# Mixture of 8: weights and biases split inside the router, identity products, one-row memset moved

## The chip, the cores and the metric

The kernel runs on one core of one Trainium2 chip. The metric is the device time of one execution in microseconds; times of several runs are compared by their medians.

## The reference

Two layers of a perceiver run over 128 sequences of 32 tokens with 128 numbers each: attention to a context, self-attention with a feed-forward part, and a mixture of experts. The change concerns the last part of layer 0, a mixture of 8 experts with two chosen per token, on the layer-normalised tokens x (4096 rows, 128 columns):

```
scores = softmax(x @ gate_w.T)                       # 8 scores a token
for each of the two experts e with the largest scores, of score w:
    h  = silu((w * x) @ w1[e].T + b1[e])
    x2 = h @ w2[e].T + b2[e]
    x3 = (w * x) @ w3[e].T + b3[e]
    out += x2 * x3
out += (silu(x @ sw1.T) * (x @ sw2.T)) @ sw3.T       # shared expert
```

The result is added to the rows before normalisation. (The kernel takes x @ w1[e].T + b1[e] / w for all experts and applies w afterwards as a scale, which is why the inverted scores have to be ready before the wide products, and in two parts.)

## The kernel before, in words

All 4096 rows stay on chip as 32 tiles of 128 rows by 128 columns. The engines run programs of their own, ordered by semaphores written out by hand; there is no planner. Layer 0's mixture of 8 is `stage_moe0` (from L1742). It has a router, a short passage, and a loop over tiles.

**Start.** SyncE issues the loads: `gate` and `lower` on semaphore `g_in`, then w1, w3, the biases `braw`, and sw12, turn_m, w2, sw3, all seven on `w_in` (L1803 to L1806); then it waits, and issues the next stage's loads (L1810). VectorE works out means and inverse deviations of all rows (L102 to L112), with one square root on ScalarE (L118). GpSimd begins with a memset of one row of 3084 numbers in a buffer of the next stage (L2120), then makes a tile of ones (L2122, L2124).

**Router.** It goes in 8 groups of 4 tiles. VectorE normalises two tiles of a group (L123, called at L1960), ScalarE the other two (L1909). TensorE transposes the four (L1876), ScalarE copies them to `xf` (L1915), TensorE multiplies them by the gate (L1819, 8 columns a tile) one group behind. The transposed tiles are needed in two parts, a high part rounded to the matmul's format and the rest: GpSimd writes the high part (L2092), VectorE the low one (L1965). Two groups are in flight.

**Weights.** Weights w1, w3 and three bias rows (1024 columns each, the biases' second part in 32 partitions) are split in the same way. This starts behind the router: ScalarE rounds them (L1942, L1944), GpSimd subtracts (L2129, L2134).

**Passage.** VectorE takes the maximum of the 8 logits (L2047), subtracts it (L2049), ScalarE takes the exponential (L1946), VectorE normalises to scores (L2051 to L2057), inverts them (L2059), and lays them out in three parts (L2061 to L2065). The semaphore `st` counts these ten steps; the score is step 6. TensorE transposes the result (L1884), ScalarE copies it (L1949), GpSimd makes the first two tiles' operands (L2095, L2099), VectorE meanwhile ranks the experts of the first four tiles (L1975 to L1993). TensorE does the shared expert's first products (L1833) and the wide products of tile 0 (L1826 to L1829).

**Loop.** For each of 32 tiles TensorE transposes the hidden values (L1843), multiplies by sw3 (L1850), does the next tile's wide and shared products, and the second matrices (L1860, L1862). GpSimd sums and prepares the tile after the next.

The later mixture of 32 experts (layer 1, `stage_moe1`) has a router of the same form, and it already issues products of the identity with itself at its start and one in each group, with the helper `keep_clock` (L1687). The names of its lines: products L1687, transposes L2529, gate products L2486. Their results go to a part of the accumulator memory that nothing reads.

Of the kernel before, what the change touches and what calls it, by code (L numbers as in the profile page):

```python
# [12 lines left out]
F32 = mybir.dt.float32  # L13
# [1728 lines left out]
def stage_moe0(nc, k, w, next_loads, next_ones):  # L1742

    ED, NG, G4 = E0 * D, T // 4, 4 * E0
    with ExitStack() as ctx:
# [31 lines left out]
        next_in, row_ok = sem("next_in"), sem("row_ok")  # L1777
        H1, X3, HT, UP, ZO = 0, 2, 4, 6, 7
        X_B, L_B, R_B = 0, 2, 4
        loads = [(w1, w["w1"]), (w3, w["w3"]), (braw, w["braw"]), (sw12, w["sw12"]),   # L1780
                 (turn_m, w["turn_m"]), (w2, w["w2"]), (sw3, w["sw3"])]
        LOADED = 16 * len(loads)
# [19 lines left out]
        def _(sp):  # L1802
            sp.dma_start(gate[:, :], w["gate"]).then_inc(g_in, 16)  # L1803
            sp.dma_start(lower[:, :, :], w["lower"]).then_inc(g_in, 16)
            for dst, src in loads:
                sp.dma_start(dst[:], src).then_inc(w_in, 16)  # L1806
            sp.wait_ge(g_in, 32)
            sp.wait_ge(w_in, LOADED)
# [5 lines left out]
        def _(pe):  # L1814
# [54 lines left out]
            pe.wait_ge(g_in, 32)  # L1869
            for g in range(NG):  # L1870
                if g > 1:
                    pe.wait_ge(xf_ok, g - 1)
# [7 lines left out]
            route(NG - 1)  # L1880
            pe.wait_ge(st, 10)
            pe.wait_ge(zero_ok, 1)
            for g in range(NG):
# [9 lines left out]
            pe.wait_ge(bl_ok, 3)  # L1893
# [5 lines left out]
            wide_up(X3, 1, 0, x3_mm)  # L1899
            groups(pe, step)  # L1900

        @block.scalar
        def _(act):
# [36 lines left out]
            act.wait_ge(w_in, LOADED)  # L1940
            for n, src in enumerate((w1, w3)):
                nc.scalar.copy(wide[:, 2 * n, :], src[:, :]).then_inc(wh_ok, 1)  # L1942
            for n in range(3):
                nc.scalar.copy(bias[:, n, :], braw[:, n, :]).then_inc(bh_ok, 1)  # L1944
            act.wait_ge(st, 2)
            nc.scalar.activation(lg[:, :, :], lg[:, :, :], ACT.Exp).then_inc(ex_ok, 1)  # L1946
            for b in range(2):
                act.wait_ge(rp_mm, b + 1)
                nc.scalar.copy(rpT[:, 4 * b:4 * b + 4, :], four(R_B + b)).then_inc(rp_ok, 1)  # L1949
# [5 lines left out]
        def _(dve):  # L1955
# [69 lines left out]
            def ranking(i, t0, base):  # L2025
# [6 lines left out]
                else:  # L2032
# [5 lines left out]
                                           ALU.mult).then_inc(sh_set, 1)  # L2038
            normal(0)
            for g in range(NG):  # L2040
                if g < NG - 1:
                    normal(g + 1)
                low(g)
# [27 lines left out]
            kept(0, 0)  # L2071
            shared(0)
# [16 lines left out]
        def _(pool):  # L2089
# [30 lines left out]
            nc.gpsimd.memset(next_ones, 1.0).then_inc(row_ok, 1)  # L2120
            pool.wait_ge(row_ok, 1)
# [5 lines left out]
            for n, src in enumerate((w1, w3)):  # L2127
                pool.wait_ge(wh_ok, n + 1)
# [712 lines left out]
```

## Time and profile before

| | |
|---|---|
| median of 3 runs | 2665.84 us (2662.67 to 2671.37) |
| the profiled execution | 2661.88 us |
| its span | 2660.1 us |
| granted TensorE clock, mean | 0.966 |
| TensorE busy | 2482.2 us |
| VectorE busy | 1610.0 us |
| ScalarE busy | 1418.8 us |
| GpSimd busy | 1049.4 us |

The span goes from the first to the last instruction of the profiled execution; the execution's own time is 1.8 us longer. Times in rows count from the span's start. PE is TensorE's matmuls, DVE VectorE, ACT ScalarE, POOL GpSimd. A line of a timeline merges instructions of one kind that follow each other: start, busy time, engine, line, operation, what it writes and reads, how many; in brackets the idle time ahead and who ended it. A product of 32-bit operands stands there as two records, a transpose as one. A clock of 1.00 is 2.4 GHz, 0.50 is 1.2 GHz.

### The profile page before, as it was taken

The page shows a single profiled execution, that of the slowest core. Times are in us where ns is not written, and L with a number is a line of the kernel's source. Part 1 is how long each engine was busy: PE and PEld are TensorE (multiplying, and loading weights), DVE is VectorE, ACT ScalarE, POOL GpSimd, SP SyncE. Part 2 cuts the span into 40 slices and gives each one's busy share as a digit, 9 for nine tenths or more (in the row PEclk, how much of TensorE's full clock was granted, in tenths as well). Part 3 has the DMA queues.
Part 4 walks back from the last instruction along what each step waited for, and adds up shares of the span by engine and source line. Part 5 has one row for each costly group of instructions (what it writes and reads, how often), then busy time and mean ns, then how long its engine had stood idle before and what let it go on. Part 6 is the DMA issues. An engine that isn't in the chain of part 4 may idle for free. (4 is left out here: it accounts for less than half of the span.)

```text
span 2660.1 us, 92957 instructions
## 1 busy us (share of the span) xinstructions
PE 2482.2 (93%) x38497; PEld 2096.3 (79%) x38497; DVE 1610.0 (61%) x3115; ACT 1418.8 (53%) x3839; POOL 1049.4 (39%) x1152
## 2 busy tenths in 40 slices
PE   6999999999989999997679998999999989889999
PEld 5888888888877888885469986777777768778888
DVE  3555555555567777775655554777777747544553
ACT  3555555555556667674644444777777734422222
POOL 2333333333340000002344444666666623345555
PEclk9999999999999999998869998999999989789999
DMA  6322222222134111110020000210101010065563
GB/s 201 128 89 89 89 89 89 89 89 89 67 125 170 40 47 39 47 40 2 1 71 1 0 0 23 50 30 24 30 24 30 13 52 0 3 135 111 107 136 75
DMA packets 60190, 168.35 MB, mean 63 GB/s; under 512 B 6429, under 2 KB 20385, under 8 KB 55209
## 3 DMA queue, kind: packets, MB, share of 16 engines
q1 hardware_dynamic: 60074, 166.71, 21.2%
q8 instruction: 84, 1.38, 0.2%
q14 instruction: 32, 0.26, 0.0%
HBM read 145.18 MB, written 21.51 MB: 63 GB/s over the span
## 5 line engine op out<-in xcount | busy, mean ns | idle before, releaser
L566 POOL TENSOR_TENSOR l_probs<-l_probs,l_rden 128x1024 f32<-128x1024 f32 x128 | 242.2, 1892 | 428.8 <-DVE l_rden L424 428.8
L508 ACT ACTIVATE l_probs<-ps,l_nmax 128x257 f32<-128x257 f32 x512 | 236.0, 474 | 226.4 <-DVE l_nmax L418 226.4
L967 POOL TENSOR_TENSOR l_probs<-l_probs,l_rden 128x1024 f32<-128x1024 f32 x128 | 242.3, 1893 | 171.2 <-DVE l_rden L818 171.2
L418 DVE TENSOR_REDUCE l_nmax<-ps 128x2 f32<-128x514 f32 x256 | 165.5, 688 | 217.4 <-PE ps L303 217.4
L903 ACT ACTIVATE l_probs<-ps,l_nmax 128x257 f32<-128x257 f32 x512 | 236.0, 474 | 59.9 <-DVE l_nmax L812 59.9
L2723 POOL TENSOR_TENSOR m_hh<-m_hh,m_cb 128x512 f32<-128x512 f32 (+1 forms) x136 | 177.3, 1304 | 156.6 <-DVE m_hh L2675 138.5
L303 PE MATMUL ps<-l_ctxQ,l_q 32*128 32x257 f32 x3072 | 202.6, 392 | 7.1 <-ACT l_probs L508 6.4
L2581 ACT ACTIVATE m_sg<-ps 128x512 f32<-128x512 f32 (+1 forms) x136 | 81.3, 598 | 231.6 <-PE ps L138 230.8
L812 DVE TENSOR_REDUCE l_nmax<-ps 128x2 f32<-128x514 f32 x256 | 165.4, 688 | 61.1 <-PE ps L704 57.6
L2675 DVE TENSOR_TENSOR m_hh<-ps,m_sg 128x512 f32<-128x512 f32 (+1 forms) x136 | 94.0, 691 | 178.6 <-PE ps L138 159.0
L823 DVE COPY l_pT<-ps 128x512 f32<-128x512 f32 x256 | 164.9, 686 | 52.2 <-PE ps L713 48.0
L343 PE MATMUL ps<-l_pT,l_ctxK 128*32 128x128 f32 x6144 | 194.3, 275 | 0.8 <-DVE l_pT L461 0.8
L343 PEld LDWEIGHTS ps<-l_pT,l_ctxK 128*32 128x32 f32 x6144 | 159.9, 110 | 43.2 <-issue 42.0
L303 PEld LDWEIGHTS ps<-l_ctxQ,l_q 32*128 32x128 f32 x3072 | 145.0, 184 | 32.2 <-ACT l_probs L508 13.8
L2517 PEld LDWEIGHTS ps<-m_wd,m_hh 128*128 128x128 f32 (+1 forms) x1088 | 143.0, 193 | 26.4 <-issue 15.1
L2517 PE MATMUL ps<-m_wd,m_hh 128*128 128x128 f32 (+1 forms) x1088 | 145.4, 277 | 12.0 <-POOL m_hh L2723 12.0
L1422 POOL CAST enc_xt<-enc_xs 128x256 fp32r (+1 forms) x32 | 12.8, 401 | 364.2 <-PE ps L138 364.2
L330 PE MATMUL ps<-ident,l_probs 128*128 128x128 f32 x1024 | 139.8, 279 | 1.4 <-ACT l_U L514 1.2
L713 PE MATMUL ps<-ident,l_probs 128*128 128x128 f32 x1024 | 133.2, 273 | 0.8 <-DVE x L832 0.4
L330 PEld LDWEIGHTS ps<-ident,l_probs 128*128 128x128 f32 x1024 | 109.6, 141 | 26.9 <-issue 25.0
L521 ACT COPY l_q<-ps 128x512 f32<-128x512 f32 x96 | 56.2, 585 | 126.7 <-PE ps L253 126.7
L461 DVE COPY l_pT<-ps 128x512 f32<-128x512 f32 x128 | 88.5, 692 | 52.3 <-PE ps L330 52.3
(371 smaller groups left out, 6471.1 us busy)
## 6 DMA issues: line engine op xcount, KB each, us to landing
l_ctxQ<-in_ctx_q SPq DMA_DIRECT2D x32, 1542.0 KB, 6.5
m_cb<-combined SPq DMA_DIRECT2D x32, 768.0 KB, 13.8
enc_dash<-kept SPq DMA_DIRECT2D x32, 512.0 KB, 3.3
l_ctxT<-in_ctx_t SPq DMA_DIRECT2D x32, 385.5 KB, 3.3
l_ctxK<-in_ctx_k SPq DMA_DIRECT2D x32, 384.0 KB, 3.1
m_cb<-combined SPq DMA_DIRECT2D x16, 512.0 KB, 13.5
kept<-enc_va SPq DMA_DIRECT2D x10, 512.0 KB, 3.2
kept<-enc_qsq SPq DMA_DIRECT2D x6, 512.0 KB
```

The costliest lines, as they stand in the source:

```text
L303: last_i = nc.tensor.matmul(ps[:, S_B + hg, 0:NK], q1[r:r + N, j, c, b, :], ctxQ[r:r + N, j, c, b * NK:b * NK + NK], start=c == 0, stop=c ...
L330: last_i = nc.tensor.transpose(ps[:, T_B + kt, hg * P:hg * P + P], probs[:, b, hg, kt * P:kt * P + P], k.ident[:, :])
L343: last_i = nc.tensor.matmul(ps[N * hg:N * hg + N, O_B, c * P:c * P + P], ctxK[:, j, at_k:at_k + N], pT[:, kt, P * hg:P * hg + P], start=kt ...
L418: nc.vector.tensor_reduce(nmax[:, par, 2 * half:2 * half + 2], ps[:, S_B + 2 * half:S_B + 2 * half + 2, 0:NK], AX.X, ALU.max, negate=True) ...
L508: nc.scalar.activation(probs[:, par, hg, :], ps[:, S_B + hg, 0:NK], ACT.Exp, bias=nmax[:, par, hg:hg + 1], accum_out=den[:, par, hg:hg + 1 ...
L566: nc.gpsimd.tensor_tensor(pr, pr, rden[:, b, :, None].to_broadcast([P, HG, NK - 1]), ALU.mult).then_inc(norm_ok, 1)
L812: nc.vector.tensor_reduce(nmax[:, b, 2 * half:2 * half + 2], ps[:, S_B + 2 * half:S_B + 2 * half + 2, 0:NK], AX.X, ALU.max, negate=True).t ...
L823: nc.vector.tensor_copy(pT[:, b % 2, kt, :], ps[:, T_B + kt, :]).then_inc(pt_ok, 1)
L903: nc.scalar.activation(probs[:, b, hg, :], ps[:, S_B + hg, 0:NK], ACT.Exp, bias=nmax[:, b, hg:hg + 1], accum_out=den[:, b, hg:hg + 1]).the ...
L967: nc.gpsimd.tensor_tensor(pr, pr, rden[:, b, :, None].to_broadcast([P, HG, K_W]), ALU.mult).then_inc(norm_ok, 1)
L2517: last = nc.tensor.matmul(ps[:, ACC + g % 2, n * P:n * P + D], hh[0:rows, v % 3, n * P:n * P + P], wd[0:rows, c, :], start=c + n == 0, sto ...
L2723: nc.gpsimd.tensor_tensor(h, h, cb[0:rows, c, :], ALU.mult).then_inc(h_ok, 1)
```

## The change

All edits are in `stage_moe0`.

- w1, w3 and the biases get a semaphore of their own, `first_in`, so that they can be used before the other loads are in. The order of the loads is as before.
- TensorE issues 8 identity products ahead of the router, one at the start of each group, and 6 behind the router when step 6 of `st` is done.
- ScalarE rounds w1 behind the turned copy of group 2 and w3 behind that of group 4; only the bias b2 is rounded behind the exponential.
- GpSimd rounds the biases b1 and b3 behind its high parts of groups 2 and 3 and subtracts for w1 and w3 behind those of groups 4 and 5.
- VectorE takes the low parts two groups later, subtracts for the two biases in iterations 5 and 6, and takes the last two low parts behind the ranking.
- GpSimd's low part of b2 and the one-row memset come behind the operands of the first two tiles. TensorE waits for that low part (`b2_lo`) ahead of the loop, and for two instead of three bias parts ahead of the wide products.

```diff
+        first_loads = [(w1, w["w1"]), (w3, w["w3"]), (braw, w["braw"])]
+        loads = [(sw12, w["sw12"]), (turn_m, w["turn_m"]), (w2, w["w2"]), (sw3, w["sw3"])]
...
             pe.wait_ge(g_in, 32)
+            keep_clock(nc, k, ZO, 8)
             for g in range(NG):
+                keep_clock(nc, k, ZO, 1)
                 if g > 1:
                     pe.wait_ge(xf_ok, g - 1)
...
             route(NG - 1)
+            pe.wait_ge(st, 6)
+            pe.nop(nofuse=True)
+            keep_clock(nc, k, ZO, 6)
             pe.wait_ge(st, 10)
             pe.wait_ge(zero_ok, 1)
+            pe.nop(nofuse=True)
...
-            pe.wait_ge(bl_ok, 3)
+            pe.wait_ge(bl_ok, 2)
...
             wide_up(X3, 1, 0, x3_mm)
+            pe.wait_ge(b2_lo, 1)
             groups(pe, step)
...
                 turned(g)
-            act.wait_ge(w_in, LOADED)
-            for n, src in enumerate((w1, w3)):
-                nc.scalar.copy(wide[:, 2 * n, :], src[:, :]).then_inc(wh_ok, 1)
-            for n in range(3):
-                nc.scalar.copy(bias[:, n, :], braw[:, n, :]).then_inc(bh_ok, 1)
+                if g == 2:
+                    act.wait_ge(first_in, FIRST)
+                    nc.scalar.copy(wide[:, 0, :], w1[:, :]).then_inc(wh_ok, 1)
+                if g == 4:
+                    nc.scalar.copy(wide[:, 2, :], w3[:, :]).then_inc(wh_ok, 1)
             act.wait_ge(st, 2)
             nc.scalar.activation(lg[:, :, :], lg[:, :, :], ACT.Exp).then_inc(ex_ok, 1)
+            nc.scalar.copy(bias[:, 1, :], braw[:, 1, :]).then_inc(b2_hi, 1)
...
+            def bias_low(n, done):
+                dve.wait_ge(bh_ok, done)
+                nc.vector.tensor_tensor(bias[N:2 * N, n, :], braw[N:2 * N, n, :], bias[N:2 * N, n, :].bitcast(F32),
+                                        ALU.subtract).then_inc(bl_ok, 1)
+
             normal(0)
             for g in range(NG):
                 if g < NG - 1:
                     normal(g + 1)
-                low(g)
+                if g > 1:
+                    low(g - 2)
+                if g == 5:
+                    bias_low(0, 1)
+                if g == 6:
+                    bias_low(2, 2)
...
             kept(0, 0)
+            low(NG - 2)
+            low(NG - 1)
             shared(0)
...
-            nc.gpsimd.memset(next_ones, 1.0).then_inc(row_ok, 1)
-            pool.wait_ge(row_ok, 1)
+            def wide_low(n, src):
+                pool.wait_ge(wh_ok, n + 1)
+                nc.gpsimd.tensor_tensor(wide[:, 2 * n + 1, :], src[:, :], wide[:, 2 * n, :].bitcast(F32),
+                                        ALU.subtract).then_inc(wl_ok, 1)
...
             for g in range(NG):
                 high(g)
...
+                if g == 2:
+                    pool.wait_ge(first_in, FIRST)
+                    nc.gpsimd.tensor_copy(bias[:, 0, :], braw[:, 0, :]).then_inc(bh_ok, 1)
+                if g == 3:
+                    nc.gpsimd.tensor_copy(bias[:, 2, :], braw[:, 2, :]).then_inc(bh_ok, 1)
+                if g == 4:
+                    wide_low(0, w1)
+                if g == 5:
+                    wide_low(1, w3)
+            pool.wait_ge(xl_ok, 1)
+            pool.wait_ge(w_in, LOADED)
             pool.wait_ge(rp_ok, 2)
             for t in range(2):
                 tile_in(t, t)
                 turn_in(0, t, t)
+            pool.wait_ge(b2_hi, 1)
+            pool.wait_ge(xt_ok, 2)
+            pool.wait_ge(rt_ok, 2)
+            nc.gpsimd.tensor_tensor(bias[N:2 * N, 1, :], braw[N:2 * N, 1, :], bias[N:2 * N, 1, :].bitcast(F32),
+                                    ALU.subtract).then_inc(b2_lo, 1)
+            pool.wait_ge(b2_lo, 1)
+            nc.gpsimd.memset(next_ones, 1.0).then_inc(row_ok, 1)
+            pool.wait_ge(row_ok, 1)
+            pool.wait_ge(xl_ok, NG)
             groups(pool, step)
```

## Rows read from the trace of the kernel before

**Rows 1.** The page: the span, and the engines' busy time.
```profile
span 2660.1 us, 92957 instructions
...
PE 2482.2 (93%) x38497; PEld 2096.3 (79%) x38497; DVE 1610.0 (61%) x3115; ACT 1418.8 (53%) x3839; POOL 1049.4 (39%) x1152
```

**Rows 2.** Stretches: length, busy us by engine, TensorE clock, DMA share, GB/s.
```profile
1330.20:1331.50 1.30, 0.00 (x0) 0.00 (x0) 1.30 (x3) 0.00 (x0) 1.30 (x1) 0.50 0.26 47
1342.00:1352.00 10.00, 10.00 (x51) 10.00 (x50) 4.31 (x10) 4.85 (x11) 2.45 (x4) 0.50 0.36 96
1366.50:1370.40 3.90, 3.13 (x13) 2.76 (x14) 2.07 (x6) 1.17 (x2) 1.15 (x4) 0.50 0.00 0
...
1450.00:1500.00 50.00, 50.00 (x334) 45.06 (x333) 27.41 (x42) 21.47 (x61) 23.52 (x38) 1.00 0.00 0
2299.20:2302.00 2.80, 2.77 (x13) 2.80 (x14) 2.23 (x13) 2.14 (x4) 0.00 (x0) 0.50 0.01 3
2302.30:2303.00 0.70, 0.70 (x9) 0.70 (x8) 0.06 (x1) 0.70 (x2) 0.00 (x0) 1.00 0.00 0
```

**Rows 3.** Timeline, start of the mixture of 8: start us, busy us, engine line.
```profile
1329.35 2.66 POOL L2120 MEMSET l_ctxT<- 1x3084 f32 x1 [3.12 <-POOLq L85]
...
1330.07 1.98 DVE L106 TENSOR_SCALAR mean<-half 128x32 f32<-128x32 f32 x1
...
1333.09 1.11 DVE L123 TENSOR_SCALAR m_xn<-x,mean,rstd 128x128 f32<-128x128 f32 x4
...
1334.23 1.94 PE L1876 MATMUL ps<-ident,m_xn 128*128 128x128 f32 x8 [28.41 <-DVE m_xn L123]
```

**Rows 4.** Timeline, start of the second mixture's router.
```profile
2299.23 3.68 PE L1687 MATMUL ps<-ident 128*128 128x128 f32 x18 [1.10 <-PEq L2164]
...
2299.76 0.18 DVE L106 TENSOR_SCALAR mean<-half 128x32 f32<-128x32 f32 x1
...
2301.25 1.11 DVE L123 TENSOR_SCALAR m_xn<-x,mean,rstd 128x128 f32<-128x128 f32 x4
```

**Rows 5.** Timeline, first router: transposes, high and low parts, weight subtractions.
```profile
1336.00 0.61 POOL L2092 CAST m_xs<-m_xf 128x512 fp32r<-128x512 f32 x1 [3.38 <-ACT m_xf L1915]
...
1340.71 0.69 DVE L1965 TENSOR_TENSOR m_xs<-m_xf,m_xs 128x512 fp32r<-128x512 f32 x1 [1.41 <-POOL m_xs L2092]
1340.74 1.09 PE L1876 MATMUL ps<-ident,m_xn 128*128 128x128 f32 x4
...
1350.55 1.09 PE L1876 MATMUL ps<-ident,m_xn 128*128 128x128 f32 x4
...
1353.29 4.89 POOL L2129 TENSOR_TENSOR m_wide<-m_w,m_wide 128x1024 fp32r<-128x1024 f32 x2 [0.35 <-ACT m_wide L1942]
```

**Rows 6.** Timeline, second router: transposes of two groups.
```profile
2306.33 0.63 PE L2529 MATMUL ps<-ident,m_xn 128*128 128x128 f32 x4 [0.92 <-issue]
...
2311.57 0.60 PE L2529 MATMUL ps<-ident,m_xn 128*128 128x128 f32 x4
```

**Rows 7.** Timeline, after the router: ScalarE, VectorE and GpSimd.
```profile
1354.06 2.94 ACT L1944 CAST m_bias<-m_braw 128x1024 fp32r<-128x1024 f32 x3
...
1355.36 0.42 DVE L2049 TENSOR_TENSOR m_lg<-ps,m_mx 128x256 f32<-128x256 f32 x1
1357.02 1.28 ACT L1946 ACT_TABLE_LOAD   x1
...
1358.34 7.16 POOL L2134 TENSOR_TENSOR m_bias<-m_braw,m_bias 32x1024 fp32r<-32x1024 f32 x3
...
1359.60 1.35 DVE L2055 TENSOR_TENSOR m_lg<-m_lg,m_mx 128x256 f32<-128x256 f32 x1
1360.99 2.31 DVE L2057 TENSOR_SCALAR m_score<-m_lg 128x256 f32<-128x256 f32 x1
```

**Rows 8.** Timeline, from the turned weights to the first loop step.
```profile
1366.50 1.97 PE L1884 MATMUL ps<-ident,m_rp 128*128 128x128 f32 x8 [11.63 <-DVE m_rp L2065]
...
1376.02 1.04 PE L1843 MATMUL ps<-ident,m_z 128*128 128x128 f32 x8
```

More of the change, by code:

```diff
@@ L1777, in stage_moe0 @@
         next_in, row_ok = sem("next_in"), sem("row_ok")
+        first_in, b2_hi, b2_lo = sem("first_in"), sem("b2_hi"), sem("b2_lo")
         H1, X3, HT, UP, ZO = 0, 2, 4, 6, 7
         X_B, L_B, R_B = 0, 2, 4
-        loads = [(w1, w["w1"]), (w3, w["w3"]), (braw, w["braw"]), (sw12, w["sw12"]),
-                 (turn_m, w["turn_m"]), (w2, w["w2"]), (sw3, w["sw3"])]
-        LOADED = 16 * len(loads)
+        first_loads = [(w1, w["w1"]), (w3, w["w3"]), (braw, w["braw"])]
+        loads = [(sw12, w["sw12"]), (turn_m, w["turn_m"]), (w2, w["w2"]), (sw3, w["sw3"])]
+        LOADED, FIRST = 16 * len(loads), 16 * len(first_loads)
         both = lambda pair: ps[:, pair:pair + 2, :].rearrange("p a b -> p (a b)")
@@ L1804, in _ @@
             sp.dma_start(lower[:, :, :], w["lower"]).then_inc(g_in, 16)
+            for dst, src in first_loads:
+                sp.dma_start(dst[:], src).then_inc(first_in, 16)
             for dst, src in loads:
@@ L1807, in _ @@
             sp.wait_ge(g_in, 32)
+            sp.wait_ge(first_in, FIRST)
             sp.wait_ge(w_in, LOADED)
@@ L2126, in _ @@
                 high(g)
-            for n, src in enumerate((w1, w3)):
-                pool.wait_ge(wh_ok, n + 1)
-                nc.gpsimd.tensor_tensor(wide[:, 2 * n + 1, :], src[:, :], wide[:, 2 * n, :].bitcast(F32),
-                                        ALU.subtract).then_inc(wl_ok, 1)
-            pool.wait_ge(bh_ok, 3)
-            pool.wait_ge(wl_ok, 2)
-            for n in range(3):
-                nc.gpsimd.tensor_tensor(bias[N:2 * N, n, :], braw[N:2 * N, n, :], bias[N:2 * N, n, :].bitcast(F32),
-                                        ALU.subtract).then_inc(bl_ok, 1)
-            pool.wait_ge(bl_ok, 3)
-            pool.wait_ge(xl_ok, NG)
+                if g == 2:
[9 more added lines that the diff above has]
+            pool.wait_ge(w_in, LOADED)
             pool.wait_ge(rp_ok, 2)
```

## The prediction

> **What bounds the kernel now.** I read the page first: TensorE is busy for 93% of the span [rows 1], so time is lost only where TensorE waits or runs at its low clock. The stretches of the mixture of 8 come next. Its loop over 32 tiles keeps TensorE busy for 50.00 of 50.00 us at a granted clock of 1.00, which is 2.4 GHz [rows 2]; the change leaves the loop alone, so the loop as a whole can only start earlier or later. The router ahead of it runs at 0.50 (1.2 GHz) though TensorE is busy without a gap from 1342 to 1352 [rows 2]. So the change can act only between 1329.35, where the stage starts [rows 3], and 1376.02, the first transposes of the loop [rows 8]: 46.7 us, 1.8% of the span. Whatever it gains there passes through the loop unchanged.
>
> In the timelines the reader should see four things in those 46.7 us. GpSimd's one-row memset holds VectorE: L106 takes 1.98 us beside it [rows 3], and 0.18 us without it at the start of the second mixture [rows 4]. The router goes at 9.81 us for four groups of four tiles, 2.45 us a group, and TensorE sets that pace [rows 5]. Then ScalarE copies three biases before its exponential, and three GpSimd subtractions lie beside VectorE's L2055 and L2057 [rows 7]. Last, eight transposes of the turned weights take 1.97 us at the low clock, and 1.04 us in the loop [rows 8].
>
> **Start and identity products.** Without the memset VectorE should go as in the second mixture, where the normalised tiles follow L106 by 1.49 us [rows 4]: 1330.07 + 1.49 = 1331.56 instead of 1333.09, 1.5 us earlier [rows 3]. That gain isn't kept. TensorE now issues nine identity products before the first transposes, and waits for gate and lower (36 KB) first. They come between 1331.5, by when the queue had moved 47 GB/s for 1.30 us, or 61 KB [rows 2], and 1334.2, when TensorE ran after that same wait [rows 3]. I take 1331.6, as the bytes say. In the second mixture 13 halves of products took 2.77 us at the low clock [rows 2], so nine cost 9 x 0.43 = 3.8 us. The first transposes start at 1335.4, **1.2 us later** than 1334.23, with 2.7 us more if the gate lands last.
>
> **Router.** The products are to raise the clock; in the second mixture it was 0.50 until 2302 and 1.00 by 2302.3, 3 us after they began [rows 2, 4]. At the high clock that router needed 5.24 us for three groups, 1.75 a group [rows 6], its own product included. Taken alone this gives 7 x (2.45 - 1.75) = 4.9 us; ScalarE's two weight copies, now inside, take back 2 x 1.0 (a third of the 2.94 us of three equal copies [rows 7]). With the later start, L2049, now at 1355.36 [rows 7], would come 1.7 us earlier, or 3.7 if the copies hide in ScalarE's gaps.
>
> Against it stand the VectorE and GpSimd operations that hold each other up, as the memset did. After the first group is turned they have to fit: 6 normalisations of two tiles at 0.55 (half of 1.11 [rows 3]), 6 low parts at 0.69, 7 high parts at 0.61, and the newcomers, two GpSimd bias copies of twice the columns of a high part (2 x 1.2), two weight subtractions (4.89 together) [rows 5] and two VectorE bias subtractions. For these last there is no row; twice a low part gives 1.4 each, which I take, and the weight subtraction on GpSimd, 2.45, is the other bound. The sum is 3.3 + 4.1 + 4.3 + 2.4 + 4.9 + 2.8 = 21.8 us. The first high part comes 1.8 us after the first transposes (1336.00 and 1334.23 [rows 3, 5]), so if none of these overlap, the reduction ahead of L2049 starts at 1335.4 + 1.8 + 21.8 = 1359.0 and L2049 0.4 later, 4.1 us after its place now. Before, the same sum without newcomers and with two low parts more was 13 us of 20, so it did not show. Between -1.7 and +4.1 I take **+1.6**, somewhat nearer the late end: L2057 waited for most of a subtraction [rows 7], but not every pair will meet.
>
> **Exponential.** The bias copies leave ScalarE's path. L2049 ends at 1355.78; a table load of 1.28 and the exponential (an estimate: 0.42, like L2049 of the same shape) could end at 1357.5, and end at 1358.7 now [rows 7]: **-1.2 us**. The third bias is copied behind it, while ScalarE waits for the weights anyway.
>
> **VectorE chain.** With GpSimd idle L2055 and L2057 should take 0.42 us like the subtraction L2049 of the same shape, instead of 1.35 and 2.31: **-2.8 us** [rows 7]. What this needs is that GpSimd's weight subtractions are over by about 1360. If not, up to 2.45 us of it is given back.
>
> **Six more products and the tail.** From the end of L2057 to the transposes of the weights are 3.2 us [rows 7, 8], and six products at 0.43 take 2.6, so they are hidden, even at the low clock. The high clock would save 0.9 us in the transposes, as much in the eight shared products behind, and 7 x 0.2 in the wide ones: 3.3 us. But GpSimd must first make four pieces (1.5 us) and the third bias's low part (2.4 us, a third of 7.16 [rows 7]), for which TensorE newly waits; these come 3.9 us after the copies of the turned weights, and the two postponed low parts of VectorE (1.4 us) can hold them up. That caps it at 3.0. Before, transposes and shared products did not raise the clock between 1366.5 and 1370.4 [rows 2]. Between 0 and -3.0 I take **-1.5**.
>
> The memset, now behind the first tiles, stands before GpSimd's piece for the third tile, which TensorE wants one loop step later; its 2.66 us cost nothing as long as a step of about 8 us lies between. Its row serves a later stage. Queue order on the DMA queue is unchanged; a split semaphore costs nothing. That the first three loads land in time is not shown by a row; if late they would stall ScalarE and GpSimd after group 2.
>
> **Sum:** +1.6 - 1.2 - 2.8 - 1.5 = -3.9 us. The profiled execution took 2661.88, and would take 2658.0. The median of the runs shown is 2665.84, 4.0 above the profiled one, so I forecast **2661.9**. A measurement here can tell about 0.3%, 8.0 us, from no change; the forecast is half of that.
>
> **Rivals.** *Strict port.* The row shows L2057 at 2.31 us beside three subtractions of 2.4 each, in order. If every such meeting costs the whole operation, the router term is +4.1 and the sum -1.4: 2664.4. The Trainium skill (SBUF — State Buffer, "Who interferes with whom") states this: whichever of the two engines issues first holds the shared ports for the whole instruction, the other is blocked fully. The 1.98 us of L106 agree. By that page alone this rival would be the forecast. Against it: the engines have gaps in which such operations lie side by side without meeting.
>
> *Free router.* The clock rises, ports seldom meet, the tail gains all: -1.7 - 1.2 - 2.8 - 3.0 = -8.7, 2657.1; with ScalarE's copies hidden -10.7, 2655.1. For it speaks the second router's pace; against it that that router had no weights to split.
>
> *Slower: low clock in the router.* The route products have only 8 columns, in the second mixture 32, and TensorE at 100% busy did not raise the clock before. If it stays at 0.50, every group costs 0.43 more, 3.0 in seven, on top of the start's 1.2; GpSimd's subtractions then reach into VectorE's chain and the 2.8 are not gained, and two blocked normalisations add 2: +4.2 + 2.0 - 1.2 = +5.0, 2670.8. It decides from the point where the first transposes show 0.50 and GpSimd still splits weights when L2055 wants to start.
>
> *Nothing.* The terms cancel, or the new wait for the third bias becomes the last: 2665.8.
>
> **How the numbers follow.** Forecast 0.42, strict port 0.23, free router 0.20, low clock 0.10, nothing 0.05. The range goes from 2654.5, which holds the free router, to 2669.5, short of the full low-clock case; the three runs shown alone differ by 8.7 us. Faster by over 0.3% needs the free router: 0.15 of its 0.20, and 0.05 for scatter of the medians: 0.20. Slower by over 0.3%: the worst of the low-clock case and scatter, 0.06. Same: 0.74.
>
> **What the new profile would show.** L106 at 0.2 us; nine identity products ending about 1335.4; clock 1.00 in the router; L2049's counterpart near 1357; weight subtractions over before L2055's counterpart, which takes 0.42; the exponential 1.75 us after L2049. Wrong would be: pairs of normalisations of over 2 us or a clock of 0.50 in the router (slower), or a router that ends before 1354 (faster), and a loop step that no longer takes the same time.

## The result and the profile after

| | before | after |
|---|---|---|
| median of 20 runs each | 2667.65 us (2662.67 to 2674.38) | 2660.64 us (2655.51 to 2667.70) |
| ratio of the medians | | 0.9972, 95% interval 0.9963 to 0.9981 |
| the profiled execution | 2661.88 us | 2664.27 us |
| its span | 2660.1 us | 2662.5 us |
| stage time, as defined below | 46.55 us | 40.42 us |

The change gains 7.5 us (5.1 to 9.9; the ratio's distance from 1 times 2667.65). The forecast was 3.9. On the page of the changed kernel the span and the busy times answer to [rows 1]:

```profile
span 2662.5 us, 93048 instructions
...
PE 2487.3 (93%) x38541; PEld 2098.8 (79%) x38541; DVE 1615.4 (61%) x3117; ACT 1416.3 (53%) x3837; POOL 1049.9 (39%) x1152
```

Whoever compares the two spans alone reads a loss of 2.4 us. The stage began at 1335.12 in this execution and at 1329.35 in the one before [rows 3], so 5.8 us of difference arose ahead of it, where both programs are the same. That is why everything below is read inside the stage, of one profiled execution a kernel. How well two executions agree there is seen on b_bias below, whose program is that of the kernel before up to the router's end: its marks up to there are the same to 0.01 us. "Stage time" runs from VectorE's memset of the scores' operand (1335.25 here, 1329.47 before) to the loop's first transposes (1375.67 here, 1376.02 before [rows 8]): it is 6.1 us less. The loop passes this on unchanged, as the prediction said. Its 32nd transposes, of which the lines stand here for before and after, come 252.55 and 252.54 us after its first:

```profile
1628.57 1.04 PE L1843 MATMUL ps<-ident,m_z 128*128 128x128 f32 x8
```

```profile
1628.21 1.03 PE L1847 MATMUL ps<-ident,m_z 128*128 128x128 f32 x8
```

From there to the second mixture's first transposes the profile before shows 674.2 us and the one after 676.9, though the programs are the same in that part too; that is where the two spans lose the gain again. Over all the kernels below this part took 674.2 to 681.2 us. The clock changes in it lie elsewhere in each profile; why stays open.

The timeline of the changed kernel through the stage, with the columns of the earlier timelines, answers to [rows 3, 5, 7, 8]:

```profile
1335.91 0.18 DVE L106 TENSOR_SCALAR mean<-half 128x32 f32<-128x32 f32 x1
...
1337.30 1.11 DVE L123 TENSOR_SCALAR m_xn<-x,mean,rstd 128x128 f32<-128x128 f32 x4
...
1337.40 4.21 PE L1687 MATMUL ps<-ident 128*128 128x128 f32 x18 [25.80 <-DMA m_lower<-in_m_lower]
...
1341.40 0.92 PE L1882 MATMUL ps<-ident,m_xn 128*128 128x128 f32 x4
...
1350.28 2.35 POOL L2146 TENSOR_TENSOR m_wide<-m_w,m_wide 128x1024 fp32r<-128x1024 f32 x1
1350.31 2.86 DVE L1977 TENSOR_TENSOR m_xs<-m_xf,m_xs 128x512 fp32r<-128x512 f32 x1
...
1353.20 1.51 DVE L2053 TENSOR_TENSOR m_bias<-m_braw,m_bias 32x1024 fp32r<-32x1024 f32 x1
1353.61 3.31 POOL L2146 TENSOR_TENSOR m_wide<-m_w,m_wide 128x1024 fp32r<-128x1024 f32 x1
...
1354.75 2.80 DVE L123 TENSOR_SCALAR m_xn<-x,mean,rstd 128x128 f32<-128x128 f32 x2
...
1357.66 1.08 PE L1882 MATMUL ps<-ident,m_xn 128*128 128x128 f32 x4 [5.15 <-issue]
...
1359.38 1.28 ACT L1957 ACT_TABLE_LOAD   x1
...
1362.45 0.42 DVE L2071 TENSOR_TENSOR m_lg<-ps,m_mx 128x256 f32<-128x256 f32 x1
1362.91 0.42 ACT L1957 ACTIVATE m_lg<-m_lg 128x256 f32<-128x256 f32 x1 [2.25 <-DVE m_lg L2071]
...
1364.20 0.42 DVE L2077 TENSOR_TENSOR m_lg<-m_lg,m_mx 128x256 f32<-128x256 f32 x1
1364.66 0.29 DVE L2079 TENSOR_SCALAR m_score<-m_lg 128x256 f32<-128x256 f32 x1
...
1365.10 2.90 PE L1687 MATMUL ps<-ident 128*128 128x128 f32 x12 [3.14 <-DVE m_score L2079]
...
1368.01 1.70 PE L1894 MATMUL ps<-ident,m_rp 128*128 128x128 f32 x8
...
1371.70 1.28 ACT L1930 ACT_TABLE_LOAD   x1 [1.36 <-PE ps L1837]
...
1372.67 2.40 POOL L2172 TENSOR_TENSOR m_bias<-m_braw,m_bias 32x1024 fp32r<-32x1024 f32 x1 [0.17 <-POOL m_rt L2123]
...
1375.13 2.67 POOL L2175 MEMSET l_ctxT<- 1x3084 f32 x1
...
1375.67 1.03 PE L1847 MATMUL ps<-ident,m_z 128*128 128x128 f32 x8
```

L106 no longer waits (0.18 us), but nine identity products fill the time before the first transposes. The router runs well up to 1350. Then VectorE's low part takes 2.86 us beside GpSimd's first weight subtraction, then the first bias subtraction 1.51, and the last pair of normalised tiles 2.80 beside the second; TensorE has no tile to turn for 5.15 us. Behind the router nothing is held up: L2077 and L2079 take 0.42 and 0.29 us, where L2055 and L2057 took 1.35 and 2.31 [rows 7].

The stretches of the changed kernel, with the columns of [rows 2]:

```profile
1342.10:1355.60 13.50, 10.26 (x88) 9.67 (x86) 12.47 (x16) 9.97 (x21) 11.31 (x10) 1.00 0.44 148
1355.70:1369.00 13.30, 8.19 (x37) 7.89 (x38) 11.06 (x18) 3.22 (x4) 2.39 (x3) 0.50 0.18 55
1369.30:1375.00 5.70, 4.60 (x26) 3.71 (x25) 2.60 (x6) 4.30 (x11) 4.33 (x5) 1.00 0.00 0
```

The clock is up from 1342.0 and down again in the long wait, so the last group and the score chain are at 1.2 GHz. VectorE is busy for 12.47 of the first 13.50 us, the time in which GpSimd holds it included: in the router it, not TensorE, now has the fewest gaps.

### The profile page after: what moved, and what is told of

The parts are those of the page before. It is cut to its first block and busy times, and to the rows that moved or that the text cites. A ratio compares the mean times of both kernels' runs of the same rounds, so it can differ in the third digit from the quotient of the medians.

```text
span 2662.5 us, 93048 instructions
## 1 busy us (share of the span) xinstructions
PE 2487.3 (93%) x38541; PEld 2098.8 (79%) x38541; DVE 1615.4 (61%) x3117; ACT 1416.3 (53%) x3837; POOL 1049.9 (39%) x1152
```

## The experiments

All times in this table are us from the start of the stage as defined above. "T" is the first transposes, "router" the end of the last gate products, "sub" the start of the subtraction of the maximum, "score" the end of the scores, "turn" the first transposes of the turned weights, "loop" the first transposes of the loop. The ratio is that of the medians against the kernel before.

| kernel | T | router | sub | score | turn | loop | ratio (95%) |
|---|---|---|---|---|---|---|---|
| before | 4.8 | 25.4 | 25.9 | 33.8 | 37.0 | 46.6 | |
| after | 6.2 | 26.7 | 27.2 | 29.7 | 32.8 | 40.4 | 0.9972 (0.9963 to 0.9981) |
| b_memset | 3.2 | 23.8 | 24.3 | 32.3 | 35.5 | 44.6 | 0.9994 (0.9979 to 1.0009) |
| b_ident | 6.2 | 29.2 | 29.7 | 37.7 | 41.0 | 47.9 | 0.9992 (0.9977 to 1.0008) |
| b_memset_ident | 6.0 | 29.0 | 29.5 | 37.5 | 40.8 | 47.7 | 0.9998 (0.9984 to 1.0012) |
| b_low_late | 6.2 | 19.2 | 19.7 | 28.9 | 32.2 | 41.0 | 0.9976 (0.9963 to 0.9989) |
| b_bias | 4.8 | 25.4 | 25.9 | 29.3 | 37.2 | 46.6 | 1.0003 (0.9989 to 1.0016) |
| a_noident | 3.2 | 25.7 | 26.2 | 28.7 | 31.7 | 40.5 | 0.9979 (0.9967 to 0.9990) |
| a_early | 3.6 | 25.6 | 26.1 | 28.6 | 31.7 | 39.5 | 0.9983 (0.9969 to 0.9996) |
| a_port | 6.0 | 19.4 | 22.2 | 25.6 | 28.7 | 37.6 | 0.9971 (0.9958 to 0.9984) |
| port_noident | 3.2 | 23.3 | 23.8 | 26.3 | 29.2 | 38.2 | 0.9982 (0.9970 to 0.9994) |
| both_moved | 3.6 | 16.4 | 20.2 | 22.7 | 25.8 | 33.4 | 0.9957 (0.9942 to 0.9973) |
| both2 | 3.6 | 16.5 | 17.0 | 20.6 | 23.7 | 30.9 | 0.9954 (0.9938 to 0.9970) |
| both2_silu | 3.7 | 16.5 | 17.0 | 20.6 | 23.7 | 30.9 | 0.9953 (0.9937 to 0.9970) |

The ratios' intervals are up to 0.33% wide, 8.8 us, so two versions are told apart by the marks of their stages; the ratio only says whether the gain arrives at the end.

### One part alone, on the kernel before

**b_memset: the one-row memset moved.**

```diff
-            nc.gpsimd.memset(next_ones, 1.0).then_inc(row_ok, 1)
-            pool.wait_ge(row_ok, 1)
             nc.gpsimd.memset(one[:, :], 1.0)
...
                 turn_in(0, t, t)
+            pool.wait_ge(xt_ok, 2)
+            pool.wait_ge(rt_ok, 2)
+            nc.gpsimd.memset(next_ones, 1.0).then_inc(row_ok, 1)
+            pool.wait_ge(row_ok, 1)
```

> The kernel before with only the one-row memset moved behind the operands of the first two tiles. Stage means here from its first operation on VectorE or GpSimd to the first transposes of the loop: 46.7 us before, 40.6 after. Theory (the memset held VectorE by 1.5 us and nothing else starts later): stage 45.2, time 1.5 us less, not to be told from no change in the total. Rival (the gate load or the clock hides it): 46.7. Second rival: the memset at its new place delays the third tile and the loop: over 47.

Every mark from the first transposes on is 1.6 us earlier, the loop 2.0. At its new place the memset costs nothing.

**b_ident: the identity products, 8 ahead, one a group, 6 behind the router.**

```diff
             pe.wait_ge(g_in, 32)
+            keep_clock(nc, k, ZO, 8)
             for g in range(NG):
+                keep_clock(nc, k, ZO, 1)
...
             route(NG - 1)
+            pe.wait_ge(st, 6)
+            pe.nop(nofuse=True)
+            keep_clock(nc, k, ZO, 6)
             pe.wait_ge(st, 10)
             pe.wait_ge(zero_ok, 1)
+            pe.nop(nofuse=True)
```

> The kernel before with only the 8, the one per group and the 6 identity products. Theory: first transposes 1.4 us later (6.3 us after the stage's start instead of 4.9), router at 1.00 clock and 1.55 to 1.75 us a group instead of 2.45, so the subtraction behind the router comes 4 to 5 us earlier than now, and the tail loses another 1.9; stage about 41, total 5 to 6 us less. Rival (the clock is raised by chance of timing or not kept with 8-column products): clock 0.50 in the router, stage 48 or more.

The stage is 1.3 us longer; I had expected it 5 to 6 us shorter. The timeline of this kernel at its second and third group, and under it two stretches, show why:

```profile
1336.63 0.60 PE L1878 MATMUL ps<-ident,m_xn 128*128 128x128 f32 x4
...
1337.91 0.69 DVE L1971 TENSOR_TENSOR m_xs<-m_xf,m_xs 128x512 fp32r<-128x512 f32 x1 [3.75 <-POOL m_xs L2098]
...
1338.52 0.94 DVE L123 TENSOR_SCALAR m_xn<-x,mean,rstd 128x128 f32<-128x128 f32 x2
...
1339.56 0.94 PE L1878 MATMUL ps<-ident,m_xn 128*128 128x128 f32 x4 [0.92 <-issue]
```

```profile
1336.40:1339.60 3.20, 2.26 (x19) 1.86 (x18) 1.69 (x4) 2.61 (x6) 1.23 (x2) 1.00 0.88 351
1339.90:1354.00 14.10, 14.10 (x68) 14.10 (x67) 5.71 (x16) 6.03 (x13) 3.08 (x5) 0.50 0.39 104
```

The clock rises 6.9 us after the stage's start and falls again at 10.3: each group's normalisation stands behind a low part on VectorE (L1971 before L123), so TensorE waits 0.92 us for the third group. After that TensorE has no gap in 14.10 us and still stays at 0.50. The products have cost 1.4 us ahead of the first transposes and lengthen every group, so the router ends 3.8 us later (29.2 against 25.4). Behind it they pay: the clock is up again from 41.0, where the turned weights' transposes start, and from there to the loop this kernel needs 6.9 us, the kernel before 9.5.

**b_memset_ident: both.**

> The kernel before with the memset moved and the identity products, while weights and biases are still split behind the router. Theory (the products wait for the gate and cover the memset): no better than the products alone, stage about 41, and the shorter ScalarE path and free VectorE chain of the whole change are missing but its blocked seventh normalisation too. Rival (the parts add up): 1.5 us better than the products alone, 39.5.

The loop comes 0.15 us earlier than with the products alone (47.7, where 41 was expected). The memset's gain is covered by the products, as the prediction's first term says.

**b_low_late: both, and the low parts two groups later.**

```diff
                     normal(g + 1)
-                low(g)
+                if g > 1:
+                    low(g - 2)
...
             kept(0, 0)
+            low(NG - 2)
+            low(NG - 1)
             shared(0)
...
-            pool.wait_ge(xl_ok, NG)
+            pool.wait_ge(xl_ok, 1)
             pool.wait_ge(rp_ok, 2)
...
+            pool.wait_ge(xl_ok, NG)
             groups(pool, step)
```

> The run with memset and identity products alone, and in addition VectorE's low parts two groups later, as in the whole change (the last two behind the ranking). In the run with products alone the clock rose before group 1 and fell 3.4 us later, when the transposes of group 2 had stood 0.9 us behind a normalisation that waited behind a low part. Theory (the later low parts are what lets the products keep the clock): clock 1.00 through the router, 1.55 us a group, last transposes 16 to 17 us after the start instead of 24.8, stage 38 to 40 instead of 47.7, although weights and biases are still split behind the router. Rival (the clock falls anyway, or the split behind the router takes it back): stage 45 or more.

The router ends at 19.2 instead of 29.0. Timeline of three groups' transposes and the end of the router in this kernel, then its stretches:

```profile
1341.01 0.60 PE L1878 MATMUL ps<-ident,m_xn 128*128 128x128 f32 x4
...
1342.56 0.60 PE L1878 MATMUL ps<-ident,m_xn 128*128 128x128 f32 x4
...
1347.22 0.60 PE L1878 MATMUL ps<-ident,m_xn 128*128 128x128 f32 x4
...
1347.65 1.90 PE L1819 MATMUL ps<-m_gate,m_xf 128*128 128x8 f32 x16
```

```profile
1337.70:1351.20 13.50, 11.85 (x106) 11.60 (x104) 8.29 (x20) 11.78 (x24) 8.55 (x9) 1.00 0.40 132
1351.40:1368.20 16.80, 7.80 (x31) 7.00 (x32) 10.59 (x16) 5.47 (x7) 12.72 (x10) 0.50 0.15 43
```

A group takes 1.55 us against 2.45 [rows 5], and the clock stays at 1.00 to the router's end. The identity products and the order on VectorE are one edit in two places: the products without the later low parts lose 1.3 us, with them (and the memset) they give 5.6. That is almost the whole gain of the change, by other means: this kernel still has the slow exponential and the slow chain (9.2 us from sub to score, against 2.5 in the kernel after), which is also why its loop starts at 41.0 and not at the 38 to 40 expected. The later low parts without the products were not run in this order of the work. In port_noident below, which has later low parts and no products, the router ends at 23.3, only 0.5 us before that of b_memset, so most of this gain needs both.

**b_bias: the three biases rounded behind the exponential.**

```diff
+            act.wait_ge(st, 2)
+            nc.scalar.activation(lg[:, :, :], lg[:, :, :], ACT.Exp).then_inc(ex_ok, 1)
             for n in range(3):
                 nc.scalar.copy(bias[:, n, :], braw[:, n, :]).then_inc(bh_ok, 1)
-            act.wait_ge(st, 2)
-            nc.scalar.activation(lg[:, :, :], lg[:, :, :], ACT.Exp).then_inc(ex_ok, 1)
```

> The kernel before with the rounding of the three biases behind the exponential, nothing else. Theory (the exponential's table load starts as soon as ScalarE is free, ahead of the wait for the logits): exponential ends 1.2 us after the start of the subtraction of the maximum or sooner (0.9 in the kernel after, 3.4 before); the score chain then runs beside GpSimd's weight subtractions and is blocked there, the bias subtractions end where they ended before; stage 44 to 45.5 instead of 46.6. Rival (the load waits for the logits): 1.75 us or more from subtraction to the end of the exponential.

Timeline of this kernel behind its router:

```profile
1359.72 1.28 ACT L1944 ACT_TABLE_LOAD   x1
...
1360.90 0.42 DVE L2049 TENSOR_TENSOR m_lg<-ps,m_mx 128x256 f32<-128x256 f32 x1
1361.35 0.42 ACT L1944 ACTIVATE m_lg<-m_lg 128x256 f32<-128x256 f32 x1 [0.35 <-DVE m_lg L2049]
...
1362.65 1.37 DVE L2055 TENSOR_TENSOR m_lg<-m_lg,m_mx 128x256 f32<-128x256 f32 x1
...
1364.68 7.16 POOL L2134 TENSOR_TENSOR m_bias<-m_braw,m_bias 32x1024 fp32r<-32x1024 f32 x3 [0.94 <-ACT m_bias L1946]
...
1367.19 2.44 DVE L2063 COPY m_rp<-m_rhi 128x512 f32<-128x512 f32 x1
1369.56 2.55 DVE L2065 TENSOR_TENSOR m_rp<-m_inv,m_rhi 128x256 f32<-128x256 f32 x1
```

The table load begins 1.18 us before L2049 does, so the exponential ends 0.87 us after that start instead of 3.37, and the scores come 4.5 us earlier. All of it is lost again, where I had expected the loop 1 to 2.5 us earlier: the same three GpSimd subtractions now lie beside L2063 and L2065, which take 2.44 and 2.55 us instead of 0.43 and 0.42, and the turned weights come no earlier (37.2). In this order of the work the exponential's gain reaches the loop only together with the removal of those subtractions.

### One part of the kernel after changed

**a_noident: without the identity products.**

```diff
-            keep_clock(nc, k, ZO, 8)
             for g in range(NG):
-                keep_clock(nc, k, ZO, 1)
...
-            pe.wait_ge(st, 6)
-            pe.nop(nofuse=True)
-            keep_clock(nc, k, ZO, 6)
             pe.wait_ge(st, 10)
             pe.wait_ge(zero_ok, 1)
-            pe.nop(nofuse=True)
```

> The kernel after without its identity products. Theory: first transposes 3.4 us after the start instead of 6.3, router at 0.50 and 2.45 us a group, its end set by the operations of VectorE and GpSimd that block each other; subtraction behind the router 26 to 28 us after the start (27.3 after), tail 1.9 us slower; stage 41 to 43. Rival (the products carry most of the gain): stage 45 or more, total like the kernel before.

Its stretches:

```profile
1342.00:1352.00 10.00, 10.00 (x51) 10.00 (x50) 6.25 (x10) 7.72 (x16) 6.94 (x7) 0.50 0.51 202
1352.00:1373.50 21.50, 12.47 (x55) 11.70 (x55) 16.71 (x25) 6.47 (x10) 8.74 (x10) 0.50 0.19 49
```

At the low clock in both stretches, with TensorE busy for 10.00 of 10.00 us in the first, the loop starts at 40.5, as it does with the products. In the whole change they are worth nothing: they make the first seven groups faster, and the faster groups then wait for VectorE. At the router's end they have cost 1.0 us (26.7 against 25.7), at the turned weights 1.1, and from there to the loop, with 7.7 us against 8.9, they give it back.

**a_early: the eight products ahead of the wait for the gate.**

```diff
-            pe.wait_ge(g_in, 32)
             keep_clock(nc, k, ZO, 8)
+            pe.wait_ge(g_in, 32)
```

> The kernel after with its first 8 identity products ahead of the wait for the gate instead of behind it. Theory: products start 2.2 us earlier, first transposes 4.0 us after the start instead of 6.2; but the first three loads still land 9.6 us after the start, ScalarE and GpSimd wait for them behind group 2, and the blocked seventh normalisation stays; stage 39.5 to 40.4. Rival (the start passes through to the end): 38.2.

The first transposes come 2.5 us earlier, the loop only 0.9: ScalarE then reaches its weight copy before w1, w3 and the biases have landed, and stands for 2.12 us; TensorE gets its next tile 2.04 us late and the clock falls at 10.1. The rest of the router goes at 0.50, and the last group now waits only 0.71 us for VectorE: what one engine no longer loses, the other does.

**a_port: the weight subtractions behind the high parts of groups 5 and 7 (instead of 4 and 5), the bias subtractions behind the router's normalisations, the low parts from the fourth on one iteration later, and so one more of them behind the ranking.**

```diff
-                if g == 4:
-                    wide_low(0, w1)
                 if g == 5:
-                    wide_low(1, w3)
+                    wide_low(0, w1)
+            wide_low(1, w3)
...
-                if g > 1:
+                if 1 < g < 5:
                     low(g - 2)
-                if g == 5:
-                    bias_low(0, 1)
-                if g == 6:
-                    bias_low(2, 2)
+                if g > 5:
+                    low(g - 3)
+            bias_low(0, 1)
+            bias_low(2, 2)
...
             kept(0, 0)
+            low(NG - 3)
```

> The kernel after with the operations on the shared port in another order: VectorE normalises the last group ahead of its low parts and of both bias subtractions, GpSimd's two weight subtractions come behind the high parts of groups 5 and 7 instead of 4 and 5. In the kernel after, the seventh pair of normalisations waits behind a bias subtraction and a weight subtraction, TensorE stands 5.2 us before its last group, and the clock falls. Theory (that blocking is what ends the router): last transposes 17 us after the start instead of 22.4, clock 1.00 until then, subtraction of the maximum 21 to 22 instead of 27.2, stage 34 to 35 instead of 40.4, total 5 to 6 us less than after (ratio to before 0.995). Rival (something else, ScalarE or the loads, ends the router; or the second weight subtraction now blocks the score chain): stage 38 to 40.

**port_noident: the same without the products.**

> a_port without any identity product. The products gave nothing in the whole change (stage 40.5 without, 40.4 with). Theory (they gave nothing only because the port ended the router): now the low clock ends it; first transposes 3.2, last ones 3.2 + 7 x 2.45 = 20.3 after the start, subtraction 25.2, stage 39 to 40, so 5 us worse than a_port. Rival (they are worth nothing in either order): stage as a_port.

Of a_port the timeline at the router's end:

```profile
1346.92 4.80 DVE L2053 TENSOR_TENSOR m_bias<-m_braw,m_bias 32x1024 fp32r<-32x1024 f32 x2
...
1347.33 3.31 POOL L2147 TENSOR_TENSOR m_wide<-m_w,m_wide 128x1024 fp32r<-128x1024 f32 x1
1347.56 1.90 PE L1823 MATMUL ps<-m_gate,m_xf 128*128 128x8 f32 x16
...
1351.74 0.42 DVE L2069 TENSOR_REDUCE m_mx<-ps 128x32 f32<-128x256 f32 x1
```

The router ends 7.3 us earlier than in the kernel after (19.4 against 26.7). That settles that the order of VectorE's and GpSimd's operations ended it there. It does not divide the 7.3 us between the two operations held by weight subtractions and the bias subtraction that stood between them, since a_port moves both. I had expected the loop at 34 to 35 and it came at 37.6, because the two bias subtractions, 4.80 us beside a weight subtraction, now stand before the reduction: L2069 starts 2.3 us after the products' end. Against port_noident the products are worth 3.8 us at the router's end and 0.7 at the loop. I had expected 5 there; the rival, that they are worth nothing in either order, was nearer. In port_noident the subtraction of the maximum starts 0.5 us behind the router's end, in a_port 2.7, so the bias subtractions take back 2.2 us, and the chain behind costs a_port another 1.0 (3.5 us from sub to score against 2.5).

### A version that goes further

**both_moved:** the edits of a_early and a_port, with ScalarE's weight copies behind groups 4 and 6 instead of 2 and 4, and GpSimd's bias copies behind groups 3 and 4 instead of 2 and 3. The first loads are then in when they are wanted.

> Both: the port order of a_port and the products ahead of the gate, with the weight and bias copies of ScalarE and GpSimd one to two groups later, so that they do not wait for the loads. Theory: the gains add, first transposes at 4.0, last ones at 15, subtraction at 19 to 20, stage 32 to 33, total about 7 us less than after (ratio to before 0.9945). Rival (the second weight subtraction runs beside the score chain and takes back up to 2.4 us): 35.

The loop starts at 33.4, between the 32 to 33 expected and the rival's 35. The router ends at 16.4, but sub is at 20.2: the bias subtractions again.

**both2:** both_moved, with the bias subtractions behind the score chain.

```diff
-            bias_low(0, 1)
-            bias_low(2, 2)
...
             dve.wait_ge(g_in, 32)
+            bias_low(0, 1)
             compared(0, 0)
...
             kept(0, 0)
+            bias_low(2, 2)
...
-            pe.wait_ge(bl_ok, 2)
+            pe.wait_ge(bl_ok, 1)
...
+            pe.wait_ge(bl_ok, 2)
             wide_up(X3, 1, 0, x3_mm)
```

> As the run with both moves (stage 33.4), with VectorE's two bias subtractions behind the last step of the score chain instead of behind the router, where they held the reduction of the maximum by 3 us. Theory: subtraction of the maximum at 17 to 18 instead of 20.2 after the start; the second weight subtraction of GpSimd now reaches into the score chain and takes back up to 1.5; stage 31 to 32, ratio to before 0.995. Rival (the bias subtractions are late for the wide products, which start 1.1 us or more later behind the turned weights): 33.4 or more.

Timeline of both2 from the end of its router to the first loop step:

```profile
1349.47 2.08 PE L1823 MATMUL ps<-m_gate,m_xf 128*128 128x8 f32 x16
...
1352.74 2.34 POOL L2148 TENSOR_TENSOR m_wide<-m_w,m_wide 128x1024 fp32r<-128x1024 f32 x1
...
1353.87 1.50 DVE L2076 TENSOR_TENSOR m_lg<-m_lg,m_mx 128x256 f32<-128x256 f32 x1
...
1365.98 1.09 PE L1847 MATMUL ps<-ident,m_z 128*128 128x128 f32 x8
...
1368.07 0.71 PE L1854 MATMUL ps<-m_sw,m_sh 128*128 128x128 f32 x4 [1.00 <-DVE m_sh L2011]
```

The loop starts 9.5 us earlier than in the kernel after; 1.3 us of it goes back in the first step, which takes 9.46 us instead of 8.14: TensorE waits 1.00 us for VectorE, which has three late low parts to do. At the 32nd transposes the lead is 8.2 us, and over both_moved 1.25 (284.74 against 285.99 from the stage's start). L2076 still waits about 1.1 us for the second weight subtraction. The median is 2652.73 us of 7 runs; the kernel before, run with it, had 2665.98. By the medians both2 is the fastest kernel here with both2_silu, but its interval (0.9938 to 0.9970) still touches that of the kernel after; the 9.5 and 8.2 us come from the two profiles.

**both2_silu:** both2, with a one-column silu on ScalarE behind the rounding of b2, so that silu's table is loaded early.

```diff
             nc.scalar.copy(bias[:, 1, :], braw[:, 1, :]).then_inc(b2_hi, 1)
+            nc.scalar.activation(sa[:, 0:1], braw[:, 1, 0:1], ACT.Silu)
```

> The run before this one with a one-column silu on ScalarE right behind the rounding of the third bias, so that the table load of 1.28 us runs there and not behind the shared products. Theory (ScalarE's silus end 0.1 to 0.3 us ahead of the wide products): silus 1.3 us earlier, stage the same within 0.3, since TensorE's wide products now end last. Rival (ScalarE's silus or what waits for them decide): 1 us less.

No difference (30.9, ratio 0.9953): what starts the loop is not silu's table.

## Why the prediction was right, and where it was off

The time was forecast at 2661.9, with a range of 2654.5 to 2669.5; 2660.64 lies in it, and the change is just under 0.3%, though the 20 runs show it to be a gain. That the forecast missed by only 1.3 us is luck in part: it started from a median of three runs that lies 1.8 us below that of the 20, and its gain was 3.1 us smaller than the difference of the medians (3.6 smaller than the ratio's 7.5). By its terms, in us of the stage:

| step | forecast | measured |
|---|---|---|
| first transposes | +1.2 | +1.4 |
| start of the subtraction of the maximum | +1.6 | +1.3 |
| from there to the end of the exponential | -1.2 | -2.5 (3.37 to 0.87) |
| to the end of the scores | -2.8 | -2.9 (4.57 to 1.63) |
| to the transposes of the turned weights | 0 | -0.1 |
| from these to the loop | -1.5 | -1.9 (9.52 to 7.66) |
| sum | -3.9 | -6.1 |

**Start and router.** The nine products eat the memset's gain, as forecast; b_memset_ident shows it from the other side. That the memset alone would give 1.5 us came out as 1.6 at the first transposes and 2.0 at the loop. In the router both halves of the argument held and nearly cancelled: the clock rose and a group took 1.55 us (forecast 1.75), and the engines that hold each other up cost it back. The forecast put the second part at anything up to the full sum of the operations. The rows show a sharper thing: little was lost in the first seven groups (from the second on, steps of 1.55 to 1.85 us), and then 5.15 us in one place, where each weight subtraction of GpSimd met one VectorE operation in the path of the last tiles, with a bias subtraction between the two. So the price was not a share of all meetings but mostly that of two, and a_port and both2 show that it can be avoided by order alone.

That +1.6 came within 0.3 us of the measured +1.3 is luck. It was chosen between two bounds, and the two sizes under it were both too small. From the first to the last transposes b_low_late, with the clock up and nothing in the way, needs 10.7 us and the kernel before 16.3, so the clock is worth 5.6, not 4.9 less 2.0 for ScalarE's copies. The kernel after needs 16.3 again: the engines that hold each other up took back 5.5, where the forecast had 3.3 (+1.6 against -1.7). The 2.0 us for ScalarE's two weight copies were not seen: in both2, which has both inside its router, the groups go at 1.55 to 1.58 us from the third on.

**Exponential: the step that failed.** The prediction says "a table load of 1.28 and the exponential could end at 1357.5", that is, the load begins when L2049 has ended. The load at 1359.38 in the kernel after came right behind ScalarE's last copy, 3.1 us before L2071 began, and b_bias, where nothing else was changed, shows the same. Before, the load stood at 1357.02 [rows 7] because the three copies ended there; L2049 had ended at 1355.78, so the row could not tell whether the load waits for both or for its engine alone, and I priced it as if for both. With the load off the path the term is 1.3 us larger, more than half of the 2.2 us missing from the sum.

**Chain.** Right in size and cause. b_bias shows the condition: with GpSimd's subtractions still there, the same chain meets them one operation later and loses everything gained.

**Products behind the router and tail.** Six products took 2.90 us and were hidden beside the reciprocal and the three operations after it, as said. The tail gave 1.9; the forecast's 1.5 was a guess between 0 and 3.0. Not all of it is the products': without them (a_noident) the tail is already 0.7 us shorter than before, since the clock rises at 37.6 there and at 44.4 in the kernel before. In the kernel after the clock rose at 1369.3, early in it: the weights' transposes (1.70 us against 1.97 [rows 8]) were still mostly at the low clock, the shared products were at the high one. The new wait for b2's low part cost nothing: it landed at 1375.07, before the last wide product had ended. The memset at 1375.13 lies beside the first loop step.

**The rivals.** The strict port foresaw a sum of -1.4 (2664.4); its mechanism is what the trace shows. The Trainium skill (SBUF — State Buffer, "Who interferes with whom") says of VectorE's two-port modes, which a copy can enter, that the engine that issues first blocks the other for its whole instruction, and of operations with two inputs that they contend with GpSimd's reads. The copy L2063 of 2.44 us, and the low part of 2.86, with two inputs, beside a subtraction of 2.35, agree. What the rival had wrong was the count: not every meeting cost its whole operation, mainly the two in the critical place did. The free router (-8.7) was wrong for this order of the work, and b_low_late shows that such a router exists: without the newcomers it ends at 19.2, and with them, in the order of a_port, at 19.4. The low clock in the router did not occur in the kernel after; it did in b_ident, from 10.3 on, and that kernel's stage was 1.3 us longer. The remark that TensorE sets the pace in the router was true before and false after, where VectorE does.

**What stays open.** The ratio says 7.5 us (5.1 to 9.9), the stage 6.1; the difference is inside the interval and no row was found for it. Likewise for both2, 15.7 in the stage, 14.4 at the loop's 32nd transposes and 12.3 by the ratio (8.0 to 16.5). In the profiles the part behind the loop was longer in most kernels whose loop ended early (681.2 us in both2, 674.2 before). Whether some of the gain is lost there or this is scatter, single profiles can't tell.

## What to carry to other kernels

Work that is moved out of a passage to stand beside other work is paid where the two engines hold each other up, so look at which operation of the critical path each moved instruction lies beside, not at the sum of busy times. Products that are to keep the clock up paid in this router only where no group had to wait: they were worth nothing in the whole change, cost 1.3 us alone, and gave 3.6 together with a later place for the low parts (b_low_late against b_memset). And an engine's load of tables needs its own line in such a sum: see whether in the rows it follows the data or only the instruction before it.

## What the runs showed of the hardware that was not expected

- **A table load can run ahead of its activation's wait, but doesn't always.** For the exponential it began 3.5 us before its input was there (1359.38 and 1362.87). For the loop's first silu (L1930) it began at 1371.70, just after the shared products had ended, and the silu followed at 1372.99, though ScalarE had been idle for 1.36 us. Why the two differ stays open.
- **Both engines lose in a meeting.** GpSimd's weight subtraction took 2.35 us as the first of a pair and 3.31 when it met VectorE's bias subtraction; its high part took 0.61 alone, up to 1.45 in a_port; VectorE's two bias subtractions took 4.80 us together there, and one took 1.22 alone. The prediction had treated such a meeting as one engine's loss.
- **TensorE busy without a gap was not TensorE at its high clock.** In a_noident it was busy for 10.00 of 10.00 us at a clock of 0.50, and in b_ident, where it issued one identity product a group besides, for 14.10 of 14.10 us. In the kernel after it was busy for 10.26 of 13.50 us and the clock was 1.00: it had risen behind the products ahead of the router and held.
- **Which VectorE operations a memset on GpSimd holds up depends on the operation.** Beside the memset before, the three additions of two inputs (L102 to L104) took 0.13 to 0.21 us (the last of them stands below), and L106, with one tensor input, 1.98 [rows 3]. L107, with two inputs, shows 1.89 right behind it, and the rows don't tell whether it was held too or only stood behind L106. The Trainium skill (SBUF — State Buffer, "Who interferes with whom") says that a two-input operation meets GpSimd's reads but not its writes, and that tensor_scalar can take both port pairs; these rows agree. In b_bias L2063, a copy, and L2065, with two inputs, both waited for subtractions, which read.

```profile
1329.82 0.21 DVE L104 TENSOR_TENSOR half<-stats 128x32 f32<-128x32 f32 x1
```
